# First FFN of a Macaron block: ScalarE's wait for the weights of all experts put behind the first turn of its job loop

## What is computed

```python
def ffn(x):                                   # x: layer norm of the residual, 1024 x 512
    scores = softmax(x @ router_w + router_b) + router_bias     # 16 experts
    # the best 2 of 4 groups of experts, in them the best 2 experts of each token
    gate = ...                                # 1024 x 16, two entries of each row are not 0
    for e in range(16):
        h = silu(x @ ew1[e] + eb1[e]) * (x @ ew2[e] + eb2[e])   # 128 wide
        y += gate[:, e:e+1] * (h @ ew3[e] + eb3[e])
    z = silu(x @ sw1 + sb1) * (x @ sw2 + sb2) @ sw3 + sb3       # shared expert, 256 wide
    return y + z
x = x + 0.5 * ffn(layernorm(x))
x = x + attention(layernorm(x))
x = x + 0.5 * ffn(layernorm(x))
```

## Time and profile before

| | us |
|---|---|
| median of 3 runs | 457.4 |
| lowest and highest run | 457.16 and 460.24 |
| the profiled execution | 461.33 |
| span of the profiled execution | 459.6 |
| mean granted TensorE clock in it | 0.965 of full |

### The profile page before, as it was taken

The page is one execution under the profiler, slowest core; times in us unless marked ns, Lnnn a source line. Parts: engine busy times, 40 slices in busy tenths (PEclk is TensorE's granted clock), DMA queues, the critical chain, the costliest instruction groups (busy, mean ns, idle before and its releaser), DMA issues.

```text
span 459.6 us, 8324 instructions
## 1 busy us (share of the span) xinstructions
PE 403.4 (88%) x2788; PEld 283.6 (62%) x2789; DVE 269.7 (59%) x695; ACT 173.8 (38%) x292; POOL 162.8 (35%) x230
## 2 busy tenths in 40 slices
PE   0899879999979979979989989979999879999973
PEld 0687567888656756655545455434587568888651
DVE  4589503232459946788886696566539932323447
ACT  1321225665302212146654354453441316556300
POOL 2511314666402853243432243243001054666400
PEclk9999997999999979999999999989999979999996
DMA  7999982544278568412213200010420042533378
GB/s 228 296 374 312 327 267 94 166 126 141 112 283 306 147 155 170 105 57 87 71 50 86 76 29 11 9 34 29 156 93 0 1 139 75 177 130 122 114 270 323
DMA packets 51180, 66.05 MB, mean 144 GB/s; under 512 B 8318, under 2 KB 30502, under 8 KB 51108
## 3 DMA queue, kind: packets, MB, share of 16 engines
q1 hardware_dynamic: 42780, 43.55, 29.9%
q0 software_dynamic: 6368, 19.32, 13.3%
q10 hardware_dynamic: 2000, 2.76, 2.1%
HBM read 46.32 MB, written 19.79 MB: 144 GB/s over the span
## 4 chain that ended last, share of the span: by engine, by line
PE 53%; DVE 18%; SPq 11%; DMA 9%; issue 5%; POOL 2%; ACT 1%; ACTq 0%; POOLq 0%; DVEq 0%
PE ps L1553 14%; PE ps L1560 7%; PE ps L1703 6%; SPq L322 5%; PE ps L1538 3%; DVE arena L1193 3%; PE ps L1622 3%; DMA w<-in_L_ffn_ew_dram 3%; PE ps L1417 3%; PE ps L1679 3%; PE ps L1651 3%; PE ps L1653 2%; SPq L394 2%; SPq L345 2%; PE ps L1665 1%
## 5 line engine op out<-in xcount | busy, mean ns | idle before, releaser
L1193 DVE TENSOR_REDUCE arena<-ps 128x3 f32<-128x384 f32 x128 | 68.7, 553 | 29.1 <-PE ps L1653 26.9
L1553 PE MATMUL ps<-arena,wj 128*128 128x128 f32 x608 | 77.3, 282 | 0.0
L1553 PEld LDWEIGHTS ps<-arena,wj 128*128 128x128 f32 x608 | 74.4, 199 | 1.0 <-issue 1.0
L800 ACT ACTIVATE arena<-ps 128x768 f32<-128x768 f32 x64 | 51.2, 810 | 52.3 <-PE ps L1667 52.1
L627 POOL TENSOR_SCALAR_AFFINE_SELECT arena<-arena 128x512 f32<-128x512 f32 x64 | 41.0, 640 | 79.2 <-ACT arena L800 78.8
L1090 DVE SCALAR_TENSOR_TENSOR arena<-ps,arena 128x128 f32<-128x128 f32 x38 | 13.3, 351 | 92.1 <-ACT arena L713 84.6
L1417 PE MATMUL ps<-arena,turns 128*128 128x256 f32 x256 | 57.6, 381 | 0.0
L559 POOL DMA_INDIRECT y_dram<-arena x38 | 38.4, 1011 | 42.3 <-DVE arena L1097 31.9
L1417 PEld LDWEIGHTS ps<-arena,turns 128*128 128x128 f32 x256 | 48.1, 190 | 8.3 <-issue 2.1
L554 POOL DMA_INDIRECT arena<-xn_dram,arena x34 | 33.2, 978 | 52.1 <-DVE arena L1030 25.2
L1560 PE MATMUL ps<-w,arena 128*128 x76 | 40.1, 611 | 4.6 <-DVE arena L1090 4.6
(11 more groups left out here) (198 smaller groups left out, 604.6 us busy)
## 6 DMA issues: line engine op xcount, KB each, us to landing
arena<-y_dram SPq DMA_DIRECT2D x16, 512.0 KB, 7.9
arena<-q_dram SPq DMA_DIRECT2D x36, 128.0 KB, 2.6
xn_dram<-arena SPq DMA_DIRECT2D x16, 256.0 KB, 6.1
w<-in_L_ffn_ew_dram SPq DMA_DIRECT2D x4, 1024.0 KB, 11.0
q_dram<-arena SPq DMA_DIRECT2D x16, 192.0 KB, 2.6
x<-_attn_hidden_states_dram SPq DMA_DIRECT2D x4, 512.0 KB, 6.3
out_dram<-x SPq DMA_DIRECT2D x8, 256.0 KB, 5.2
arena<-arena SPq DMA_DIRECT2D x30, 64.0 KB
```

Of the source, the lines that this page charges most:

```text
L800: act.activation(pr[:, n % 2, pair, :], ps[:, bank:bank + 2, :].rearrange("p a b -> p (a b)")[:, 0:768], ACT.Exp).then_inc(sem("exp"), 1)
L1193: dve.tensor_reduce(m3[:, h:h + 1, :], ps[:, bank, 0:3 * P].rearrange("p (n k) -> p n k", n=3), AX_X, ALU.max).then_inc(sem("s_max"), 1)
L1553: ins = pe.matmul(o, wj[:, par, c, n * INTER:(n + 1) * INTER], xgT[:, par, c, :], start=(c == 0), stop=(c == KC - 1))
```

## The change

ScalarE's loop body is written as a function `two_jobs(i)`. In the first FFN its first turn (i = 0) is written out ahead of the loop; the wait for all groups stands behind it, and the loop then runs from 1. In the second FFN the loop runs from 0 as before and there is no wait. VectorE counts the groups that are needed at once by the expert of job 4, not of job 2.

```diff
             weights_copy(2, 0, first[2])
-            if f == 0:
-                for g in range(1, E // EG):
-                    act.wait_ge(sem(f"ew_in{g}"), 49)
-            with act.Fori(0, rest + 1) as i:
+
+            def two_jobs(i):
+
                 e3 = expert(2 * i + 3)
                 silu(2 * i + 1, 1)
                 gather_copy(2 * i + 3, 1)
...
                 silu(2 * i + 2, 0)
                 gather_copy(2 * i + 4, 0)
                 weights_copy(2 * i + 4, 0, e4)
+
+            if f == 0:
+                two_jobs(0)
+                for g in range(1, E // EG):
+                    act.wait_ge(sem(f"ew_in{g}"), 49)
+            with act.Fori(1 - f, rest + 1) as i:
+                two_jobs(i)
             silu(2 * rest + 3, 1)
...
-                link(dve.tensor_tensor(later[:], iota[0:1, EG:E:EG], bc(jexf[0:1, 2:3], [1, E // EG - 1]), ALU.is_le))
+                link(dve.tensor_tensor(later[:], iota[0:1, EG:E:EG], bc(jexf[0:1, 4:5], [1, E // EG - 1]), ALU.is_le))
```

## The result

The changed kernel took 454.27 us (median of 22 runs, 450.11 to 458.54). The kernel before, run beside it, took 459.28 us, and not the 457.4 us of its first three runs. The ratio is 0.9886, with a 95% interval of 0.9862 to 0.9910: 5.2 us or 1.1% faster, where 7.1 us were forecast. The ratio leaves out the runs that are more than 1.5% above the fastest of their kernel, here three of the 22. The time lies 0.27 us above the stated range. The profiled execution took 450.85 us with a span of 449.1 us; it is one of the fastest of the 22.

The account below looks back on a forecast made before the run. TensorE, busy 88% of the span, was taken to bound the kernel, except where the chain ran through the last expert weights' load. 4.18 + 2.91 + 0 = 7.09 us off 457.4 gave 450.3 us; range 447.4 to 454.0.

Parts of the forecast that it names:

- The wait moved: First FFN: job 1's down product starts on TensorE at 65.74 and not at 69.92 us, a gain of 4.18 us.
- The clock: First FFN, from job 1's down product to job 2's: the half clock after TensorE's idle time goes, a gain of 2.91 us.
- It moves as a block: Everything behind the first FFN's jobs starts from their end, so the gain of 7.09 us lasts to the end.
- Late next: Wait's new place, before job 3's SiLU: costs about 0.05 us; weights may land by 70.04 us for nothing, cover 2.0 us.
- transfers: Scatter of job 0 and gather 6 are issued earlier; cost taken as 0, upper bounds 0.8 and 1.2 us.
- count: VectorE's count to job 4: no group but the first is needed up to job 7, so no cost.
- code: ScalarE's program gets 14 instructions outside its loops, issued under running copies; cost 0, the second FFN likewise.
- Rival 1: First FFN: the clock's part does not come; gain 4.18 us, 453.2 us; chance 0.10.
- Rival 2: Another clock fall goes too, as that after 163.55 us; gain 10.0 us, 447.4 us; chance 0.06.
- Rival 3: The wait takes hold at its new place, weights landing 4 us later; cost 2.0 us, 452.3 us; chance 0.04.
- Rival 4: Counted wait before the first weight copy grows if job 4's expert is 12 or more; 5.4 slower, 462.8 us; chance 0.02.
- Rival 5: ScalarE's code is fetched in all 8 turns of the second FFN's loop; 11.7 us in all, 462.0 us; chance 0.02.

Follow-up runs that it names:

- x1_turn_out_wait_stays: The changed kernel with the wait for all groups put back ahead of the written-out turn; 459.9 us, ratio 0.9987.
- a1_again: The changed kernel, unchanged, profiled once more; 456.55 us, ratio 0.9915.
- k1_filled_wait: The kernel before with 18 unused matmuls on TensorE between job 2's up and job 1's down product in the first FFN; 458.41 us, ratio 0.9969.
- b1_again: The kernel before, unchanged, built again and profiled once more; 461.91 us, ratio 1.005.
- b2_again: The kernel before, unchanged, profiled a third time; 460.32 us.
- lb_before_late_group: The kernel before with one more 1 MB transfer on SyncE's queue ahead of the last weight group's loads; 461.52 us, ratio 1.0043.
- la_after_late_group: The changed kernel with one more 1 MB transfer on SyncE's queue ahead of the last weight group's loads; 457.73 us, ratio 0.9890.

## Why the prediction was right and wrong

*The wait moved: right in place and kind, too large.* The SiLU of job 1 follows its product, TensorE does not stand, and nothing waits at the new place. The term was 4.18 us, from the earliest possible start of job 1's down product (1.79 us after that of up product 2) to its real one. Read so, the five profiles of the table give 4.18, 3.91, 3.80, 2.98 and 2.74 us, 3.5 in the mean.

*The clock: the term that failed.* The step is "The difference, 2.91 us, is the half clock ... I count it as gained". It was read off one execution, and that one has the largest value of five (2.75, 2.58, 1.64, 0.10, 0.09; mean 1.4). It was also read in two ways at once, from the chain behind work and behind idle time, which made 2.75 into 2.91. Of the fillers' pairs, one gives 1.55 us in its profiles and one 2.25 us in its medians, so the cost is real and its size stays rough. I had written that idle times alone do not decide when the clock falls, but used this only for falls elsewhere and not for the term itself. I had also taken the start of the stand as fixed. It depends on when the rows of jobs 0 and 1 land and on how early the front of the FFN is, while the landing of the weights stays at 67.7 to 69.1 us. A late start took from the first term each time, and came with no fall of the clock in two profiles and with one in x1_turn_out_wait_stays; what decides the fall stays open. Over all profiles, the last down product is at 121.8 us in the mean of the five of before and at 116.4 us in the mean of the changed kernel's four (116.25, 116.87, 116.40 and, kept busy, 116.11). That is 5.4 us, against 5.2 measured on the whole kernel: 3.5 and 1.4 for the two terms, and 0.4 because TensorE happened to reach job 0's down product later in the profiles of before (63.45 us in the mean) than in those of after (63.01). In the first pair of profiles the sum closes too: 4.18, less 0.29 for a later start after (66.03 and not 65.74), plus 2.75 is the 6.64 us gained.

*The base.* The time followed from 457.4 us, the median of three runs that were 3.1 us apart; 22 runs gave 459.28. Of the 3.97 us between 450.3 and 454.27, 1.88 are the base and 2.09 the two terms. I took the base without a width of its own, and that, on top of the clock's term, put the time just outside the range.

*It moves as a block: nothing speaks against it.* The filled and the unfilled pairs are 5.5 and 5.4 us apart, so theory D has no support. What follows the first FFN took 335.8 to 337.3 us in three profiles of the kernel before and 332.9 to 336.9 us in three of the changed one; the first two profiles stood at nearly opposite ends of that, which is why they differ by 10.5 us. The ranges overlap, and three profiles each do not show whether the rest of the program is also a little faster after the change.

*Late next, transfers, count, code: right as far as shown.* SiLU 3 waits for its product, the scatter and gather 6 are found in time, and x1_turn_out_wait_stays shows no effect of the count and the code (0.9987, 0.9951 to 1.0023).

*The rivals.* Rival 1 (no clock part, 4.18 us) is what some executions do, and the runs' gain of 5.2 us lies between it and the forecast; it deserved far more than 0.10, as a share of the executions and not as another world. Rival 2 (gain 10.0 us) is what the first pair of profiles shows (10.5), and the 22 runs do not bear it out. Rival 3 did not occur; with a landing 2.2 us later ScalarE did wait, but not TensorE. Rival 4 did not either: the first weight copy was at 52.33 us. Rival 5 did not: three of the changed kernel's four profiles have no "remote" pause in either FFN, and the fourth, a1_again, has one in the second FFN, not eight. The Trainium skill ("Runtime: NRT & Kernel Launch", section "Instruction fetch mechanics") says that a taken branch waits for a fetch when its target lies outside the two blocks of code that are held. By that rule the loop would not be fetched anew in each turn, and these traces agree.

## What to carry to other kernels

A wait put behind the work that does not need it gives back its whole stand, as long as that work covers it, and also the half clock that the stand may cause; count the first by how early the waiting engine arrives in several executions, and the second as a chance with a size, not as a difference read off one. Before a forecast within 1%, take the base from more runs than three, or state the gain and the base apart. And look at how much cover stands behind the new place of a wait: here 2 us more of late weights cost nothing. A distance between two steps is read in one view, the timeline: the chain's times shift with what stands before a step.

## What the runs showed that I had not expected

- ScalarE's pauses. In the job loops, and only there, a SiLU that opens a loop turn sometimes comes 1.9 to 2.6 us late, released by something that the trace calls "remote". Nine of the fourteen profiles have none, k1_filled_wait has five, and the other four have two or three; where two follow each other in one loop they are 12.8 to 13.0 us apart (81.61, 94.59 and 107.54 us above). One costs TensorE nothing to 0.6 us. The cause stays open; that they come with the code's place is not supported, since profiles of one and the same kernel differ in them. They do go with the job in which a kernel ran: all four profiles of the first job of experiments have them, and none of the eight of the other two jobs, which ran on other chips.
- Matmuls that compute nothing, put ahead of waits, made the kernel before faster (0.9938, 0.9906 to 0.9970), and the changed kernel with them has the lowest ratio of all, 0.9834 (0.9789 to 0.9878) against 0.9886 (0.9862 to 0.9910) without; the two intervals overlap a little, so the second gain is likely rather than shown. The Trainium skill ("TensorE: Matmul & The Clock Gate", section "HAM oscillation — how this bites in real kernels") describes waits between bursts that put the clock back to half and advises another loop order; the windows above agree with the effect (0.50 unfilled, 1.00 filled), and there filling the wait kept the clock up too. Two unfilled profiles of the table kept 1.00 as well.
- The same kernel, built and run again beside itself, came out at 1.005 (1.0012 to 1.0088). An interval over runs does not hold this difference.
- Equal idle times are followed by different clocks. The idle time before the attention's first turn is 2.52 us in all ten profiles that do not fill it; behind it the granted clock stayed at 1.00 in five of them (both first profiles among these) and fell to 0.50 within 2 us in the other five (b1_again, b2_again, x1_turn_out_wait_stays, lb_before_late_group, la_after_late_group).
